# How query and key parts lie in memory, and by what transfers a stack of them is read

## The reference

```python
# x: 8 batches, 128 channels, 256 positions; 16 heads of 8 components
x = x + tanh(g_xattn[0]) * conv_attention(ctx, ctx, layernorm(x))        # stage 1
x = x + tanh(g_ffn[0])   * experts32(layernorm(x))                       # stage 2
# stage 3: attention with rotary encoding
q = rotary(Wq @ layernorm(x) + bq); k = rotary(Wk @ ctx + bk); v = Wv @ ctx + bv
scores = einsum('bdhn,bdhm->bhnm', q, k) / sqrt(8)
o = einsum('bhnm,bdhm->bdhn', softmax(scores), v)
x = x + tanh(g_xattn[1]) * (Wm @ o + bm)
x = x + tanh(g_ffn[1])   * experts8(x)                                   # stage 4
```

## Time and profile before

| | |
|---|---|
| median of 3 runs | 494.24 us (487.6 to 494.79) |
| profiled execution | 491.66 us, of it 489.8 us from the first to the last instruction |
| busy, of the span | PE 84%, DVE 60%, ACT 34%, POOL 31% |
| granted TensorE clock | 0.927 of full speed |
| transfers | 43.53 MB, 49867 packets, mean 89 GB/s |

### The profile page before, as it was taken

How to read it: one execution, slowest core, us unless ns; L and a number is a source line. 1 busy time by engine, 2 the same in 40 slices (tenths; PEclk the granted TensorE clock), 3 DMA queues, 4 the chain that set the end, 5 groups by cost and what they waited for, 6 DMA issues and landing times.

```text
span 489.8 us, 7462 instructions
## 1 busy us (share of the span) xinstructions
PE 413.6 (84%) x2821; PEld 266.0 (54%) x2821; DVE 295.0 (60%) x613; ACT 166.6 (34%) x300; POOL 153.8 (31%) x234
## 2 busy tenths in 40 slices
PE   1489993869769768699998768999999989899996
PEld 1378883824535435368886534455555545465554
DVE  1859997499916454633447778688898823322212
ACT  1221320133345434200110125467767785311110
POOL 0658898248972210502111060022112231110000
PEclk9999996588859998999999869699999999899999
DMA  6692010200049999741183141543345000000101
GB/s 197 190 286 87 33 34 32 87 0 0 1 121 267 254 258 233 188 143 36 58 162 83 57 97 34 119 87 75 64 78 98 3 3 1 1 0 1 43 0 43
DMA packets 49867, 43.53 MB, mean 89 GB/s; under 512 B 4101, under 2 KB 48553, under 8 KB 49833
## 3 DMA queue, kind: packets, MB, share of 16 engines
q1 hardware_dynamic: 47264, 40.65, 32.8%
q0 software_dynamic: 800, 2.10, 1.5%
q10 hardware_dynamic: 1768, 0.33, 0.4%
HBM read 36.55 MB, written 6.32 MB: 88 GB/s over the span
## 4 chain that ended last, share of the span: by engine, by line
PE 50%; DMA 16%; POOL 13%; DVE 11%; issue 3%; SPq 3%; ACT 3%; DVEq 0%; POOLq 0%; ACTq 0%
DMA WG<-in_L_ffn_w_gate_up_dram 10%; PE PS L1038 8%; PE PS L1221 7%; PE PS L1184 6%; PE PS L1080 5%; PE PS L1007 5%; PE PS L1065 4%; PE PS L957 3%; DMA R<-qparts_d 3%; DMA X<-in_x_dram 2%; DVE MX L1457 2%; PE PS L1033 2%; POOL SA L430 2%; POOL R L491 2%; SPq L343 2%
## 5 line engine op out<-in xcount | busy, mean ns | idle before, releaser
L1457 DVE TENSOR_REDUCE MX<-PS 128x2 f32<-128x512 f32 x128 | 85.9, 709 | 18.4 <-PE PS L1007 18.0
L708 ACT ACTIVATE R<-PS 128x1024 f32<-128x1024 f32 x64 | 65.4, 1024 | 46.9 <-PE PS L1065 46.5
L1038 PE MATMUL PS<-R 128*128 128x256 bf16 x384 | 47.3, 276 | 0.0
L1007 PE MATMUL PS<-R 72*128 72x256 bf16 x192 | 39.9, 295 | 6.6 <-DVE MX L1457 5.5
L1080 PE MATMUL PS<-R 128*32 128x256 f32 x512 | 42.6, 407 | 1.4 <-ACT R L718 1.0
L1038 PEld LDWEIGHTS PS<-R 128*128 128x128 bf16 x384 | 37.9, 99 | 5.9
L411 POOL TENSOR_TENSOR RSB<-RSA,MH 128x2 f32<-128x2 f32 (+2 forms) x20 | 14.3, 713 | 75.9 <-issue 40.2
L553 POOL TENSOR_TENSOR X<-X,R 128x256 f32<-128x256 f32 x8 | 5.8, 727 | 99.9 <-ACT R L731 99.9
L957 PE MATMUL PS<-WG,R 128*64 128x352 f32 x128 | 24.0, 496 | 14.8 <-DMA WG<-in_L_ffn_w_gate_up_dram 14.2
L1221 PE MATMUL PS<-WG,R 128*128 128x256 f32 x128 | 33.1, 405 | 1.3 <-DVE R L1624 1.2
L1065 PE MATMUL PS<-R 75*128 75x256 bf16 x192 | 31.6, 290 | 1.7 <-DMA R<-MR 1.7
(11 more groups left out here) (237 smaller groups left out, 796.2 us busy)
## 6 DMA issues: line engine op xcount, KB each, us to landing
WG<-in_L_ffn_w_gate_up_dram SPq DMA_DIRECT2D x16, 704.0 KB, 12.6
WD<-in_L_ffn_w_down_dram SPq DMA_DIRECT2D x16, 352.0 KB
R<-kparts_d SPq DMA_DIRECT2D x24, 192.0 KB
R<-qparts_d SPq DMA_DIRECT2D x18, 192.0 KB
R<-kpad_d SPq DMA_DIRECT2D x1, 2048.0 KB, 7.9
kparts_d<-SA SPq DMA_DIRECT2D x4, 384.0 KB, 2.5
qparts_d<-WD SPq DMA_DIRECT2D x4, 384.0 KB, 3.2
SA<-qparts_d SPq DMA_DIRECT2D x6, 192.0 KB
```

What stands on the lines that cost most here:

```text
L708: act.activation(PX[:, G % 4].rearrange("p h m n -> p (h m n)"), PS[:, 2 * (G % 2):2 * (G % 2) + 2, :].rearrange("p a n -> p (a n)"), ACT. ...
L1007: last = pe.matmul(PS[:, 4 + H % 2, m * L:m * L + L], QST[b % NST][0:NT, h, m * P:m * P + P], KST[b % NST][0:NT, h, :], start=True, stop=True)
L1038: last = pe.matmul(o, OHT[:, k, b * P:b * P + P], Y[:, k, s, :], start=False, stop=(k == KT0 - 1 and s == 2))
L1457: dve.tensor_reduce(MX[:, H % NH, :], PS[:, 4 + H % 2, :].rearrange("p (m n) -> p m n", m=LB), AX, ALU.max).then_inc(s_max, 1)
```

## The change

Memory is laid out as [batch, part, 128 rows, 256 positions], for keys with five parts (now these hold parts 0 and 1 twice) and for queries with three. One part of one batch is contiguous, with the 16 heads of a component side by side, so a stack's row is one piece of 8 KB. A stack is read by one transfer for keys and one for queries, of 72 rows each, with a hand-built access pattern on the memory side: three blocks, 24 rows in each, 4096 elements in a row. For keys the blocks begin one part apart (`step` 8 rows of 4096 elements, so they overlap); for queries the step is 0, and the same 24 rows are read three times. The pairs of parts that the 72 rows form are the same nine. Which block has which parts is swapped between keys and queries.

```diff
+ROW = NH * L
-        kparts_d = nc.dram_tensor("kparts_d", [3, P, T * 2], BF16, kind="Internal")
-        qparts_d = nc.dram_tensor("qparts_d", [5, P, T * 2], BF16, kind="Internal")
+        kparts_d = nc.dram_tensor("kparts_d", [B, 5, P, L], BF16, kind="Internal")
+        qparts_d = nc.dram_tensor("qparts_d", [B, 3, P, L], BF16, kind="Internal")
...
             for c in range(QC):
                 sp.wait_ge(kp_parts, c + 1)
-                sp.dma_start(kparts_d.ap().rearrange("s p n -> p s n")[:, :, c * 512:c * 512 + 512],
-                             KR["parts"]).then_inc(kp_out, 16)
+                for i in range(2):
+                    to = kparts_d.ap()[2 * c + i].rearrange("s p n -> p s n")
+                    sp.dma_start(to[:, 0:3, :], KR["rows"][:, 3 * i:3 * i + 3, :]).then_inc(kp_out, 16)
+                    sp.dma_start(to[:, 3:5, :], KR["rows"][:, 3 * i:3 * i + 2, :]).then_inc(kp_out, 16)
...
-                for r in range(3):
-                    rows = slice(3 * HD * r, 3 * HD * r + 3 * HD)
-                    for dst, src, part in ((KST, kparts_d, 0), (QST, qparts_d, r)):
-                        sp.dma_start(dst[b % NST][rows, :, :],
-                                     src.ap()[part:part + 3].rearrange("s (d h) (b n) -> (s d) h b n", h=NH, b=B)[:, :, b, :])\
-                          .then_inc(st_in[b % NST], 16)
+                for dst, src, parts, step in ((KST, kparts_d, 5, HD * ROW), (QST, qparts_d, 3, 0)):
+                    rows = bass.AP(tensor=src, offset=b * parts * HD * ROW, ap=[[step, 3], [ROW, 3 * HD], [1, ROW]])
+                    sp.dma_start(dst[b % NST][0:NT, :, :].rearrange("p h n -> p (h n)"), rows)\
+                      .then_inc(st_in[b % NST], 16)
...
             def qout(c):
                 sp.wait_ge(qp_parts, c + 1)
-                cols = slice(c * 512, c * 512 + 512)
-                sp.dma_start(qparts_d.ap().rearrange("s p n -> p s n")[:, 0:3, cols], QR["parts"]).then_inc(qp_out[c], 16)
-                sp.dma_start(qparts_d.ap().rearrange("s p n -> p s n")[:, 3:5, cols], QR["parts"][:, 0:2, :])\
+                sp.dma_start(qparts_d.ap()[2 * c:2 * c + 2].rearrange("b s p n -> p (b s) n"), QR["rows"])\
                   .then_inc(qp_out[c], 16)
```

More of the change, by code:

```diff
@@ L134, in rope_views @@
         def rope_views(base):
-            return dict(a=base[:, 0:512], b=base[:, 512:1024],
-                        parts=base[:, 1024:1792].bitcast(BF16).rearrange("p (s n) -> p s n", s=3))
+            flat = base[:, 1024:1792].bitcast(BF16)
+            return dict(a=base[:, 0:512].rearrange("p (b n) -> p b n", b=2),
+                        b=base[:, 512:1024].rearrange("p (b n) -> p b n", b=2),
+                        parts=flat.rearrange("p (b s n) -> p s b n", b=2, s=3),
+                        rows=flat.rearrange("p (r n) -> p r n", n=L))
         KR = rope_views(SA[:, :, :].rearrange("p s n -> p (s n)")[:, 0:1024 + 768])
@@ L355, in qout @@
                 sp.wait_ge(qp_parts, c + 1)
-                cols = slice(c * 512, c * 512 + 512)
-                sp.dma_start(qparts_d.ap().rearrange("s p n -> p s n")[:, 0:3, cols], QR["parts"]).then_inc(qp_out[c], 16)
-                sp.dma_start(qparts_d.ap().rearrange("s p n -> p s n")[:, 3:5, cols], QR["parts"][:, 0:2, :])\
+                sp.dma_start(qparts_d.ap()[2 * c:2 * c + 2].rearrange("b s p n -> p (b s) n"), QR["rows"])\
                   .then_inc(qp_out[c], 16)
             qout(0)
-            sp.wait_ge(kp_out, 16 * QC)
-            sp.wait_ge(qp_out[0], 32)
+            sp.wait_ge(kp_out, 64 * QC)
+            sp.wait_ge(qp_out[0], 16)
             stack(0)
@@ L368, in _ @@
             maxrow(0)
-            sp.wait_ge(qp_out[1], 32)
+            sp.wait_ge(qp_out[1], 16)
             stack(2)
@@ L374, in _ @@
                 if b + 3 < B:
-                    sp.wait_ge(qp_out[(b + 3) // 2], 32)
+                    sp.wait_ge(qp_out[(b + 3) // 2], 16)
                     stack(b + 3)
@@ L483, in _ @@
                 root(2 * c, 2 * c + 2)
-            pool.wait_ge(kp_out, 16 * QC)
+            pool.wait_ge(kp_out, 64 * QC)
             def shared(u):
@@ L585, in cast @@
                 if c >= 1 and s == 0:
-                    act.wait_ge(qp_out[c - 1] if q else kp_out, 32 if q else 16 * c)
+                    act.wait_ge(qp_out[c - 1] if q else kp_out, 16 if q else 64 * c)
                 if q:
@@ L1002, in smax @@
                 if h == 0:
-                    pe.wait_ge(st_in[b % NST], 16 * 6 * (b // NST + 1))
+                    pe.wait_ge(st_in[b % NST], 16 * 2 * (b // NST + 1))
                 if H >= 2:
@@ L1299, in turn_up @@
                         dve.wait_ge(sem_parts, c)
-                    dve.scalar_tensor_tensor(out=two(R["a"]), in0=two(PS[:, b0, :]), scalar=BT[:, bias:bias + 1],
+                    dve.scalar_tensor_tensor(out=R["a"], in0=two(PS[:, b0, :]), scalar=BT[:, bias:bias + 1],
                                              in1=bc(FQ[:, 0, :], [P, 2, L], 1), op0=ALU.add, op1=ALU.mult)
-                    dve.scalar_tensor_tensor(out=two(R["b"]), in0=two(PS[:, b0 + 1, :]),
+                    dve.scalar_tensor_tensor(out=R["b"], in0=two(PS[:, b0 + 1, :]),
                                              scalar=BT[:, bias + 1:bias + 2],
@@ L1528, in qlast @@
                     dve.wait_ge(qp_parts, QC - 1)
-                dve.scalar_tensor_tensor(out=two(QR["b" if i else "a"]), in0=two(PS[:, 7, :]),
+                dve.scalar_tensor_tensor(out=QR["b" if i else "a"], in0=two(PS[:, 7, :]),
                                          scalar=BT[:, 2 + i:3 + i], in1=bc(FQ[:, i, :], [P, 2, L], 1),
```

## The result

| | before | after |
|---|---|---|
| median of 4 runs each | 490.92 us (482.79 to 494.79) | 550.76 us (546.57 to 554.42) |
| ratio, 95% interval | | 1.135 (1.115 to 1.155) |
| profiled execution | 491.66 us, span 489.8 | 547.85 us, span 545.8 |
| granted TensorE clock | 0.927 | 0.838 |

The change makes the kernel 13% slower. The forecast was 531 us, with a range of 515 to 580. So its direction and range held, and its own size was 17 to 20 us too small. Medians are of all runs of a kernel, while a ratio compares only the runs within 1.5% of its fastest, so the two can differ a little.

The account below looks back on a forecast made before the run. PE's own rounds were taken as the bound, with stacks just in time. Three engines would make the last batch's stack 32.9 us late: 491.66 + 32.9 + 6 for the clock = 530.6, so 531 us, range 515 to 580.

Parts of the forecast that it names:

- The bound: PE's own rounds from batch to batch bound the kernel; late stacks cost PE only 1.0 us, all there is to win.
- Three engines: Each stack transfer, with 3 blocks outermost in memory, is shared by 3 transfer engines instead of 12; chance 0.76 for 531 us.
- The rival of twelve engines by the 72 rows of the SBUF side: Stack transfers are dealt out by the SBUF side's 72 rows, so 12 engines share as before: 490.7 us, chance 0.11.
- The price of a piece: In the stack transfers, one 8 KB piece costs one engine 0.304 us.
- D: Time from a stack's issue to its landing: 1.6 + 14.6 + 0.5, together 16.7 us instead of 10.5.
- The rival of slow pieces: Three engines share a stack, but an 8 KB piece costs 0.50 us: 605 us, chance 0.10.
- The link: From a batch's first head on PE, over the last maxima, to SP's next stack issue: 4.1 us a round.
- The loop: Once stacks are late, each round costs 4.1 us plus the time from issue to landing: 20.8 us for batches 4 to 7.
- Place by place: Lateness summed from batch 0 (0.9 us) over the cast (3.3) and later stacks to batch 7's first head (32.9).
- The clock: PE, idle in late rounds, drops to a granted clock of 0.50; mostly hidden in the wait, together 6 us.
- The keys' writes: Keys' parts written in 512 B pieces land 4 to 4.5 us after first issue: nothing, at most 1 us in three rounds.
- What the profile would show: 3 small packets a transfer, share 0.19, some 80 GB/s, waits of some 6 us for batches 3 to 7, rounds about 21 us.

Follow-up runs that it names:

- e12: The changed kernel with the memory side's two outer counts exchanged, 24 rows outermost (twelve engines): 488.09 us, ratio 1.000 to the kernel before.
- early12: The changed kernel with 24 rows outermost and, on SP, stack(b + 3) ahead of maxrow(b + 1): 490.43 us, ratio 0.999 to the kernel before.
- the four versions: The changed kernel with its memory side's outermost count at 3 (as is), 4, 6 or 24: 550.76, 516.59, 487.96 and 488.09 us.
- early: The changed kernel, still on three engines, with stack(b + 3) ahead of maxrow(b + 1) on SP for b from 1 on: 530.33 us.
- old3: The kernel before, its layout, six transfers and 512 B pieces kept, each memory side given as three blocks outermost (three engines): 564.12 us.

## Why the prediction was right, and where its sizes were off

**The bound.** Right: it said that at most 1.0 us is to be won by faster stacks, and `e12` (1.000) and `early12` (0.999) win nothing that can be measured.

**Three engines.** Right by the count of small packets (3, 4, 6 and 12 for each transfer in the four versions), by the share of 0.19 and by 81 GB/s for 80 forecast. The Trainium skill's rule (DMA: Bandwidth & Descriptors, "Why a DMA increments its semaphore by 16 and not by 1") gives the same four numbers; here they are measured. The rival of twelve engines by the 72 rows of the SBUF side is out: those 72 rows are the same in all four versions.

**The price of a piece.** 0.304 us forecast, 0.31 by the window. D was forecast as 1.6 + 14.6 + 0.5 = 16.7 and is 17.7 to 18.3: 48 pieces in a row need some 16 us, 0.33 each with the gaps between them. The term is 1.0 to 1.6 us too small. The rival of slow pieces (0.50 us) does not hold with three engines.

**The link.** 4.1 us, 4.7 at the low clock, 5.3 in the first round; it was 4.5 to 5.0, and 5.9 in the first. The loop itself is shown by `early`.

**Place by place**, counted from the first stack's issue, in us later than before:

| place | forecast | measured |
|---|---|---|
| head of batch 0 | 0.9 | 2.7 |
| cast of the queries | 3.3 | 4.7 |
| head of batch 2 | 7.2 | 10.6 |
| head of batch 3 | 8.9 | 14.8 |
| heads of batches 4, 5, 6 | 14.1, 20.6, 26.5 | 21.7, 30.2, 38.1 |
| head of batch 7 | 32.9 | 48.1 |
| end | 38.9 | 51.6 |

The forecasts of the table hold the 6 us for the clock only in the last line. The 12.7 us that are missing: 3.4 up to the head of batch 2 (1.4 at the cast, which waits for two stacks, 1.0 more up to the issue of `stack(2)`, 1.0 by its D); 2.5 in the round from 2 to 3; 5.7 in the three middle rounds, where D is 1.0 to 1.6 us longer and the link 0.4 to 0.9 above 4.1; 3.6 in the round from 6 to 7; and 2.5 the other way behind the last stack (3.5 us measured, where I had put the 3 of slow running and the 3 of the links).

**D is the term that cost most.** It is off by little, 1.0 to 1.6 of 16.7 us, but it is paid twice at the cast and once at each of six landings: an estimate from the places above is 8 of the 12.7 us. The prediction's sentence that 1 us more on D is 6.3 us more in all is too low as well: its own two sums give (107.3 - 32.9) / (26 - 16.7) = 8.0.

**The clock** was undersized too. I wrote that a slow stretch "hides in the wait" and gave it 6 us in all. It hides only while it is shorter than the wait. In the rounds of 24.45 and 24.37 us PE was busy throughout at its lower level, so the wait was gone and PE itself was late. By an estimate with 17.7 us for D, which no wait shows in these two rounds, the stacks had landed 0.8 and 1.7 us before PE took them up. With the link's growth, 3.5 us over five rounds (forecast 3), and 3.5 us behind the last stack, the clock is worth some 10 us by this estimate. The other 22 of the 32.0 us by which PE is busy longer lie in time in which the stacks weren't there yet anyway.

**Costed at nothing.** The keys' writes: right. They go out at 43.98 to 45.45 us and land 2.2 us after their issues, so the last is there 3.7 us after the first issue (forecast 4 to 4.5); the cast that needs them, at 50.02, still waits for POOL; and `e12`, which has them all, is level with before. Fewer issues on SP: right, no gain.

**What the profile would show.** Small packets, share and bandwidth: as written. The first part is unchanged but for the 4.4 us told above. Rounds of about 21 us: they are 22.5 to 24.5. Waits of "some 6 us for each of batches 3 to 7": 7.28, 3.87 and 3.60 in three of the five, and none in the two slow rounds, though those are the longest. A list of waits alone would have understated them.

## What to carry to other kernels

Before merging transfers, read how many transfer engines each one uses (the small packets at its end, or the busy share times 16) and put a count outermost on both sides that many engines can share equally (here 24 gave twelve, 128 gave sixteen, 3 gave three): the same bytes in larger pieces with three engines cost 60 us here, and exchanging two counts of the access pattern gave them back. Then ask what the path has room for: the transfer could take 10 us of a 14 us round for nothing, and everything above that was paid once for each round, with a slower TensorE on top. When a wait is gone from the list but the round is longer, look at the granted clock of that round before calling it solved.

## What was not expected of the hardware

- A piece has no fixed price: 8 KB took 0.31 us with three, four or six engines at work (26.6, 26.5, 26.0 GB/s each), and 0.46 us with twelve (17.6 GB/s each, 206 in all). From six to twelve engines D falls only from 10.2 to 10.7 us to 8 to 9.
- From the third of six on, an issue on SP took 2.9 to 3.7 us instead of 0.8 when three engines had the 384 pieces of each transfer to take (`old3`). SP was held for about as long as three engines needed for one such transfer.
- TensorE's granted clock stayed at 0.50 for a whole round of 24.45 us in which PE was never idle, behind a wait of 5.09 us; before, the round of PE busy throughout had 1.00. PE's busy time grew by 32.0 of the 51.6 us lost, for the same multiplies, at a mean clock of 0.82 instead of 0.94. What ends such a stretch no run here isolates.
